# A mixture of experts behind two attentions: eight fixed tiles, seven looked up, and two tiles' weights loaded early

## The chip, the core and the metric

The kernel runs on one core of a Trainium2 chip. The metric is the device time of one execution in microseconds (us), and less is better. The core has TensorE (PE, matmuls and transposes), VectorE (DVE), ScalarE (ACT), GpSimd (POOL), and SyncE (SP), which issues nearly all transfers here. Each runs its own instruction list in order and meets the others at semaphores. All transfers share 16 DMA engines.

## The reference, cut to what matters

Four batches of 128 tokens with 512 features go through three stages, each added to its input: cross-attention over 2048 context rows per batch, self-attention over the 128 tokens, and a mixture of eight experts, of which each token takes two.

```python
x = x + xattn(layernorm(x), ctx_1024, ...)     # 16 heads, 2048 keys per batch
x = x + attn(layernorm(x), ...)                # 16 heads, rotary, 128 keys
x = x + ffn(layernorm(x), ...)

# ffn, xf = its input as 512 rows of 512
rn = (xf - mu) * rsqrt(var + EPS) * ln_gamma + ln_beta
probs = softmax(rn @ gate_w.T)
rw, sel = top_k(probs, 2)
comb = sum(one_hot(sel, 8) * rw[..., None], axis=1)
h = gelu(einsum('nc,efc->enf', xf, w1))        # w1: 8 x 1024 x 512
y = einsum('enf,ecf->enc', h, w2)              # w2: 8 x 512 x 1024
out = einsum('enc,ne->nc', y, comb)
```

## The kernel before

**Three stages.** `cross_attention` runs batch by batch; every engine has a loop (`Fori(0, NB - 1)`) over three batches, with semaphore counts and addresses computed in registers, and the fourth batch written out behind it. `self_attention` is written out and pipelined over the four batches. `mixture` follows it behind a block boundary.

**Tiles of the mixture.** The 1024 (token, expert) pairs are sorted by expert into slots of DRAM, `slots_in`, in tiles of 128 rows. Each expert begins a tile of its own, so 15 tiles always suffice (`TILES`). The router on VectorE works out each pair's slot (`rows`, semaphore `rowed`) and each tile's expert (`of_tile`, semaphore `tabled`). GpSimd scatters the normalised tokens with eight indirect transfers (`sent`). SyncE reads the 15 expert numbers into registers behind `tabled`, and addresses the weights with them.

**One tile k.** Its weights are 2 MB of w1 and 2 MB of w2 in float32. ScalarE makes the float16 high part (`w1_high`, `w2_high`, two instructions each) and VectorE the low part (`w1_low`, `w2_low`, two each). TensorE transposes the tile's 128 rows (`rows_transposed`, called the transposes below), and multiplies by w1 in 96 matmuls (the up part) and by w2 in 24 (the down part, `down_tile`). ScalarE applies the gelu to the up part's result, `y_evict` copies the down part's, and `y_store` sends it to `slots_out`. At the end GpSimd gathers both rows of each token, VectorE adds them, and the result is stored.

**Buffers and orders.** Raw weights, high and low parts, `rows_in`, `xT`, `h` and `y` are each double: tile k uses buffer k % 2. The order on TensorE, which the change leaves alone, is up(k), transposes(k + 1), down(k - 1). ScalarE in iteration k: w1_high(k + 1), y_evict(k - 2), gelu and high part of h for the two halves, x_high(k + 1), w2_high(k). VectorE follows it: w1_low(k + 1), the low parts of h, x_low(k + 1), w2_low(k). SyncE in iteration k, one queue:

```python
w1_load(k + 2)   # waits for w1_low(k)
rows_load(k + 2) # waits for the transposes of tile k
y_store(k - 2)   # waits for y_evict(k - 2)
w2_load(k + 2)   # waits for w2_low(k)
```

`w2_high(k)` waits for down(k - 2), which is the last reader of its buffer (`act.wait_ge(down, k - 1)`), and `y_evict(k)` for down(k). w1 and w2 of tile 0 are loaded during self-attention, and w1 of tile 0 is split there (in eight parts). w2 of tile 0 is split in the mixture.

**Lines.** SyncE: w1_load L1456, w2_load L1462, rows_load L1468, y_store L1472, output L1491. ScalarE: w1_high L1653 (the profile writes `w_hi<-w_raw`), w2_high L1661 (`cT_hi<-w_raw`: the high part of w2 lies in the old context buffer), x_high L1666, y_evict L1673, gelu L1686, high part of h L1690. VectorE: w1_low L1599, w2_low L1606 (`cT_lo<-w_raw`), x_low L1612, low part of h L1622. TensorE: transposes L1703, up L1751 to L1753, down L1734 to L1736. GpSimd: scatter L1509, gather L1517. L748 are the transposes at the start of a batch of cross-attention.

Of the kernel before, what the change touches and what calls it, by code (L numbers as in the profile page):

```python
# [16 lines left out]
P = 128  # L17
NB = 4
# [151 lines left out]
def cross_attention(nc, io, t, s):  # L170
# [19 lines left out]
    with ExitStack() as ctx:  # L190
# [103 lines left out]
        def _(sp):  # L294
# [75 lines left out]
            with sp.Fori(0, NB - 1) as b:  # L370
                one_batch(b, in_loop)
# [6 lines left out]
        def _(pool):  # L378
# [55 lines left out]
            with pool.Fori(0, NB - 1) as b:  # L434
                one_batch(b, in_loop)
# [3 lines left out]
        def _(v):  # L439
# [182 lines left out]
            with v.Fori(0, NB - 1) as b:  # L622
                one_batch(b, in_loop)
# [3 lines left out]
        def _(act):  # L627
# [109 lines left out]
            with act.Fori(0, NB - 1) as b:  # L737
                one_batch(b, in_loop)
# [3 lines left out]
        def _(pe):  # L742
# [177 lines left out]
            with pe.Fori(0, NB - 1) as b:  # L920
                one_batch(b, in_loop)
# [8 lines left out]
def self_attention(nc, io, t, s):  # L930
# [7 lines left out]
    with ExitStack() as ctx:  # L938
# [139 lines left out]
        def _(v):  # L1078
# [47 lines left out]
            def split_w1(n):  # L1126
# [3 lines left out]
                                               in0=t.w1_raw[:, c, half].rearrange("p c n -> p (c n)"), scalar=W_SCALE,  # L1130
# [83 lines left out]
        def _(act):  # L1214
# [8 lines left out]
            for step in STEPS:  # L1223
# [39 lines left out]
                if step == NB - 1:  # L1263

                    act.wait_ge(s.w1_in, 16)
                    for n in range(NF):
                        c_, half = w1_part(n)
                        nc.scalar.activation(t.w1_hi[:, c_, half], t.w1_raw[:, c_, half], ACT.Copy,
# [96 lines left out]
TILES = 2 * TOK // P + EXPERTS - 1  # L1365
# [3 lines left out]
def mixture(nc, io, t, s):  # L1369
# [3 lines left out]
    with ExitStack() as ctx:  # L1373
# [7 lines left out]
        w1_raw, w2_raw = [t.w1_raw, sb("w1_raw1", [P, NC, FF])], [t.w2_raw, sb("w2_raw1", [P, NF, D])]  # L1381
# [13 lines left out]
        counting = sb("m_counting", [P, TILES + NB * EXPERTS])  # L1395
# [4 lines left out]
        n_tiles, ends, starts = sb("m_n_tiles", [P, EXPERTS]), sb("m_ends", [P, EXPERTS]), sb("m_starts", [P, EXPERTS])  # L1400
        ones, over = sb("m_ones", [P, EXPERTS]), sb("m_over", [P, TILES, EXPERTS - 1])
        place, placed = sb("m_place", [P, NB, EXPERTS]), sb("m_placed", [P, 2, NB, EXPERTS])
        rows_f, of_tile_f = sb("m_rows_f", [P, 2, NB]), sb("m_of_tile_f", [P, TILES])
        rows = sb("m_rows", [P, 2, NB], mybir.dt.uint32)
        of_tile = sb("m_of_tile", [P, TILES], mybir.dt.int32)
        tile_no, rank = counting[:, 0:TILES], counting[:, TILES:].rearrange("p (b e) -> p b e", e=EXPERTS)

# [10 lines left out]
        w1_in, w2_in = [s.w1_in, sem("m_w1_in1")], [s.w2_in, sem("m_w2_in1")]  # L1418
# [27 lines left out]
        def _(sp):  # L1446
# [3 lines left out]
            sp.wait_ge(tabled, 1)  # L1450
            expert = [0] + [sp.value_load(of_tile[0:1, k:k + 1], min_val=0, max_val=EXPERTS - 1) for k in range(1, TILES)]

            def w1_load(k):
                if k >= 2:
                    sp.wait_ge(w1_lo_s, w1_parts(k - 2))
                sp.dma_start(w1_raw[k % 2][:, :, :], io.w1[bass.ds(expert[k], 1), :, :, :].rearrange("e p c n -> (e p) c n")  # L1456
                             ).then_inc(w1_in[k % 2], 16)

            def w2_load(k):
                if k >= 2:  # L1460
                    sp.wait_ge(w2_lo_s, PARTS * (k - 1))
                sp.dma_start(w2_raw[k % 2][:, :, :], io.w2[bass.ds(expert[k], 1), :, :, :].rearrange("e p c n -> (e p) c n")  # L1462
                             ).then_inc(w2_in[k % 2], 16)
# [405 lines left out]
```

## Time and profile before

| | us |
|---|---|
| median of 3 runs | 1163.97 |
| lowest, highest | 1159.47, 1173.82 |
| the profiled execution's own time | 1163.01 |
| its span, first to last instruction | 1161.1 |

| engine | busy us | share of the span |
|---|---|---|
| TensorE matmul | 950.7 | 82% |
| VectorE | 727.9 | 63% |
| ScalarE | 527.1 | 45% |
| GpSimd | 281.6 | 24% |
| DMA engines, mean (q1, which SyncE feeds) | | 33.9% |

Shares are averages over three stages: cross-attention takes the first 780 us, self-attention goes to 890, and the mixture takes the last 271 us. Times within the span are counted from its start, and what lies outside it is 1163.01 - 1161.1 = 1.9 us. The granted clock of TensorE averages 0.919 over the span.

### The profile page before, as it was taken

How to read it: one execution, taken by the hardware profiler on the slowest of the kernel's cores; microseconds unless marked ns; L12 is line 12 of the kernel's file. 1: busy time of each engine (PE TensorE's matmuls, PEld its weight loads, DVE VectorE, ACT ScalarE, POOL GpSimd, SP SyncE). 2: the span in 40 equal slices, each digit the busy share in tenths (PEclk: the TensorE clock that was granted, in tenths of full speed). 3: DMA queues.
4: the chain of work that ended last, by engine and by line, in shares of the span. 5: the costliest groups of instructions: out<-in, count | busy, mean ns of one | idle time of the engine just before them, and what ended most of it. 6: DMA issues, size and time to landing. Idle time of an engine off the chain costs nothing. (4 is left out here: it accounts for less than half of the span.)

```text
span 1161.1 us, 21099 instructions
## 1 busy us (share of the span) xinstructions
PE 950.7 (82%) x8057; PEld 529.9 (46%) x8057; DVE 727.9 (63%) x1066; ACT 527.1 (45%) x790; POOL 281.6 (24%) x244
## 2 busy tenths in 40 slices
PE   5899988889998889999889998757865078888871
PEld 4554444544443544444444444333443066555550
DVE  7965466683655673656683456775764277778772
ACT  4343444434344433344543344433453167778770
POOL 2610444320333410034530033442311200000002
PEclk9899998899999689999999999679977579999996
DMA  6333222032322013412123312218000558899844
GB/s 244 96 91 80 69 56 56 2 105 62 91 56 54 3 58 89 106 30 51 37 66 114 77 31 52 67 47 307 1 1 4 205 225 349 345 352 353 345 184 126
DMA packets 48531, 136.10 MB, mean 117 GB/s; under 512 B 9708, under 2 KB 11500, under 8 KB 44600
## 3 DMA queue, kind: packets, MB, share of 16 engines
q1 hardware_dynamic: 47160, 130.58, 33.9%
q0 software_dynamic: 1280, 4.20, 1.2%
q8 instruction: 71, 1.16, 0.4%
q14 instruction: 20, 0.16, 0.0%
HBM read 96.96 MB, written 11.04 MB: 93 GB/s over the span
## 5 line engine op out<-in xcount | busy, mean ns | idle before, releaser
L561 DVE TENSOR_REDUCE mpart<-ps_r 128x1 f32<-128x512 f32 x192 | 127.0, 687 | 96.1 <-PE ps_r L858 95.8
L693 ACT ACTIVATE pT<-ps_s 128x1024 f32<-128x1024 f32 x128 | 128.3, 1020 | 95.0 <-PE ps_s L880 91.3
L429 POOL TENSOR_TENSOR acc_pool<-acc_pool,pT 128x1024 f32<-128x1024 f32 x60 | 143.3, 2388 | 9.7 <-POOL acc_pool L429 5.5
L895 PE MATMUL ps_o<-pT,vals 128*32 128x128 f32 x2048 | 108.5, 305 | 24.3 <-ACT pT L693 24.0
L429 POOL TENSOR_TENSOR acc_pool<-pT 128x1024 f32<-128x1024 f32 x16 | 38.2, 2390 | 293.2 <-ACT pT L693 278.8
L554 DVE TENSOR_TENSOR k_lo<-k_f,k_hi 128x512 f16<-128x512 f32 x64 | 43.9, 688 | 103.8 <-ACT k_hi L715 103.8
L1751 PE MATMUL ps_h<-m_xT_hi,w_hi 128*128 128x128 f16 x480 | 84.9, 224 | 24.2 <-DVE m_xT_lo L1612 24.2
L769 PE MATMUL ps_r<-wv_hi,cT_hi 128*128 128x512 f16 x256 | 99.6, 389 | 6.0 <-DVE cT_lo L469 5.7
L839 PE MATMUL ps_r<-cT_hi,wk_hi 128*128 128x512 f16 x256 | 97.3, 380 | 5.1 <-DVE mpart L561 4.7
L710 ACT ACTIVATE k_f<-ps_r,kbias 128x512 f32<-128x512 f32 x64 | 43.9, 686 | 123.2 <-PE ps_r L841 120.7
L770 PE MATMUL ps_r<-wv_lo,cT_hi 128*128 128x512 f16 x256 | 99.2, 388 | 0.0
L771 PE MATMUL ps_r<-wv_hi,cT_lo 128*128 128x512 f16 x256 | 98.9, 386 | 0.0
L858 PE MATMUL ps_r<-k_stack,q_stack 98*128 98x512 f16 x192 | 84.1, 438 | 16.9 <-DVE mpart L561 12.7
L841 PE MATMUL ps_r<-cT_hi,wk_lo 128*128 128x512 f16 x256 | 97.0, 379 | 0.0
L840 PE MATMUL ps_r<-cT_lo,wk_hi 128*128 128x512 f16 x256 | 97.0, 379 | 0.0
L636 ACT ACTIVATE vals<-ps_r 128x512 f32<-128x512 f32 x64 | 38.2, 597 | 121.5 <-PE ps_r L771 121.5
L880 PE MATMUL ps_s<-q_stack,k_stack 98*128 (+1 forms) x1024 | 89.8, 233 | 2.2 <-ACT q_stack L720 2.2
L1752 PE MATMUL ps_h<-m_xT_lo,w_hi 128*128 128x128 f16 x480 | 84.7, 224 | 0.0
L1753 PE MATMUL ps_h<-m_xT_hi,w_lo 128*128 128x128 f16 x480 | 84.7, 224 | 0.0
L880 PEld LDWEIGHTS ps_s<-q_stack,k_stack 98*128 98x128 f16 x1024 | 70.8, 104 | 30.2 <-issue 21.3
L1599 DVE SCALAR_TENSOR_TENSOR w_lo<-w_raw,w_hi 128x2048 f16<-128x2048 f32 x28 | 62.9, 2288 | 31.0 <-ACT w_hi L1653 31.0
L895 PEld LDWEIGHTS ps_o<-pT,vals 128*32 128x32 f32 x2048 | 49.5, 116 | 69.6 <-issue 34.4
(233 smaller groups left out, 1849.3 us busy)
## 6 DMA issues: line engine op xcount, KB each, us to landing
w_raw<-in_w SPq DMA_DIRECT2D x30, 2048.0 KB, 10.1
raw<-in_context SPq DMA_DIRECT2D x64, 256.0 KB, 2.8
k_stack<-k_hi SPq DMA_DIRECT2D x256, 64.0 KB, 2.0
k_stack<-k_lo SPq DMA_DIRECT2D x128, 64.0 KB, 2.0
slots_in<-a_zeros SPq DMA_DIRECT2D x1, 3840.0 KB, 24.6
rows_in<-slots_in SPq DMA_DIRECT2D x15, 256.0 KB, 12.9
slots_out<-m_y SPq DMA_DIRECT2D x15, 256.0 KB, 10.5
q_stack<-k_stack SPq DMA_DIRECT2D x12, 128.0 KB, 2.3
```

Source lines behind the costliest of these rows:

```text
L429: nc.gpsimd.tensor_tensor(acc_pool[:, :], pT[:, 0, :] if p == 1 else acc_pool[:, :], pT[:, p % PT, :], ALU.add).then_inc(pool_add, 1)
L561: nc.vector.tensor_reduce(mpart[:, j, kb:kb + 1], p1_bank(step, n - 1), AX.X, ALU.max).then_inc(p1_max, 1)
L693: nc.scalar.activation(pT[:, p % PT, :], ps_s[p % 2][:, :], ACT.Exp, scale=SM_SCALE).then_inc(exp_done, 1)
L769: nc.tensor.matmul(bank[:, :], cT_hi[:, c, keys], t.wv_hi[:, c, :], start=(c == 0), stop=False)
L770: nc.tensor.matmul(bank[:, :], cT_hi[:, c, keys], t.wv_lo[:, c, :], start=False, stop=False)
L771: last = nc.tensor.matmul(bank[:, :], cT_lo[:, c, keys], t.wv_hi[:, c, :], start=False, stop=(c == NC - 1))
L839: nc.tensor.matmul(bank[:, :], t.wk_hi[:, c, col], cT_hi[:, c, keys], start=(c == 0), stop=False)
L840: nc.tensor.matmul(bank[:, :], t.wk_hi[:, c, col], cT_lo[:, c, keys], start=False, stop=False)
L841: last = nc.tensor.matmul(bank[:, :], t.wk_lo[:, c, col], cT_hi[:, c, keys], start=False, stop=(c == NC - 1))
L880: last = nc.tensor.matmul(ps_s[p % 2][:, at:at + P], t.k_stack[g % 2][0:ROWS, j, P * kt:P * (kt + 1)], t.q_stack[0:ROWS, HPG * g + j, bass ...
L895: last = nc.tensor.matmul(ps_o[g % 2][HD * j:HD * (j + 1), 0:P], vals[:, 2 * p + i, head:head + HD], pT[:, p % PT, at:at + P], start=(p == ...
L1751: nc.tensor.matmul(to, w1_hi[u][:, c, col], xT_hi[u][:, c, :], start=(c == 0), stop=False)
```

## The change

There are still 15 tiles. Tiles 0 to 7 now belong to experts 0 to 7, fixed when the kernel is built, and only tiles 8 to 14 (`MORE` = 7) are looked up: an expert with over 128 pairs has its further tiles there. The router's arithmetic for a pair's slot gets four more small instructions (one on 8 values, three on 32), and its table of experts 7 entries instead of 15.

The weights of tiles 0 and 1 are loaded during self-attention, behind the zeroing of `slots_in` (before: those of tile 0, ahead of it). In the mixture ScalarE splits w2(0), w1(1) and w2(1) early, in between the router's steps. ScalarE's order in iteration k is now y_evict(k - 2), w2_high(k), gelu, x_high(k + 1), w1_high(k + 2); VectorE's is w2_low(k), low parts of h, x_low(k + 1), w1_low(k + 2). SyncE issues w1(2) and w2(2) before the rows, w1(3) and w2(3) behind rows 0 and 1, then reads the seven expert numbers, and in iteration k loads rows of tile k + 2, w1 of tile k + 4, stores y of tile k - 2, and loads w2 of tile k + 4. The order on TensorE is as it was.

The loop over three batches of cross-attention is written out on all five engines. The diff, cut:

```diff
...
-            with pe.Fori(0, NB - 1) as b:
+            for b in range(NB - 1):
                 one_batch(b, in_loop)
...
             sp.dma_start(t.gate[:, :, :], io.gate).then_inc(s.gate_in, 16)
-            sp.dma_start(t.w1_raw[:, :, :], io.w1[0:1, :, :, :].rearrange("e p c n -> (e p) c n")).then_inc(s.w1_in, 16)
-            sp.dma_start(t.w2_raw[:, :, :], io.w2[0:1, :, :, :].rearrange("e p c n -> (e p) c n")).then_inc(s.w2_in, 16)
             sp.wait_ge(zeroed, 1)
             sp.dma_start(io.slots_in.rearrange("(n p) d -> p n d", p=P),
                          zeros[:, :].unsqueeze(1).broadcast_to([P, TILES, D])).then_inc(s.slots_zeroed, 16)
+            for e in range(2):
+                sp.dma_start(t.w1_raw[e][:, :, :], io.w1[e:e + 1, :, :, :].rearrange("e p c n -> (e p) c n")
+                             ).then_inc(s.w1_in[e], 16)
+                sp.dma_start(t.w2_raw[e][:, :, :], io.w2[e:e + 1, :, :, :].rearrange("e p c n -> (e p) c n")
+                             ).then_inc(s.w2_in[e], 16)
...
-TILES = 2 * TOK // P + EXPERTS - 1
+MORE = 2 * TOK // P - 1
+TILES = EXPERTS + MORE
...
-            sp.wait_ge(tabled, 1)
-            expert = [0] + [sp.value_load(of_tile[0:1, k:k + 1], min_val=0, max_val=EXPERTS - 1) for k in range(1, TILES)]
+            expert = list(range(EXPERTS))
+
+            def experts_of_further_tiles():
+                sp.wait_ge(tabled, 1)
+                expert.extend(sp.value_load(of_tile[0:1, k:k + 1], min_val=0, max_val=EXPERTS - 1) for k in range(MORE))
+
+            def weights_of(w, k):
+                e = expert[k]
+                return (w[e:e + 1, :, :, :] if k < EXPERTS else w[bass.ds(e, 1), :, :, :]).rearrange("e p c n -> (e p) c n")
 
             def w1_load(k):
-                if k >= 2:
-                    sp.wait_ge(w1_lo_s, w1_parts(k - 2))
-                sp.dma_start(w1_raw[k % 2][:, :, :], io.w1[bass.ds(expert[k], 1), :, :, :].rearrange("e p c n -> (e p) c n")
-                             ).then_inc(w1_in[k % 2], 16)
+                sp.wait_ge(w1_lo_s, w1_parts(k - 2))
+                sp.dma_start(w1_raw[k % 2][:, :, :], weights_of(io.w1, k)).then_inc(w1_in[k % 2], 16)
 
             def w2_load(k):
-                if k >= 2:
-                    sp.wait_ge(w2_lo_s, PARTS * (k - 1))
-                sp.dma_start(w2_raw[k % 2][:, :, :], io.w2[bass.ds(expert[k], 1), :, :, :].rearrange("e p c n -> (e p) c n")
-                             ).then_inc(w2_in[k % 2], 16)
+                sp.wait_ge(w2_lo_s, PARTS * (k - 1))
+                sp.dma_start(w2_raw[k % 2][:, :, :], weights_of(io.w2, k)).then_inc(w2_in[k % 2], 16)
 
             def rows_load(k):
                 if k >= 2:
@@ -1471,19 +1480,23 @@
                 sp.wait_ge(y_out, k + 1)
                 sp.dma_start(io.slots_out[P * k:P * (k + 1), :], y[k % 2][:, :]).then_inc(y_sent[k % 2], 16)
 
-            w1_load(1)
-            w2_load(1)
+            w1_load(2)
+            w2_load(2)
             sp.wait_ge(sent, 16 * 2 * NB)
             rows_load(0)
             rows_load(1)
+            w1_load(3)
+            w2_load(3)
+            experts_of_further_tiles()
             for k in range(TILES):
                 if k + 2 < TILES:
-                    w1_load(k + 2)
                     rows_load(k + 2)
+                if k + 4 < TILES:
+                    w1_load(k + 4)
                 if k >= 2:
                     y_store(k - 2)
-                if k + 2 < TILES:
-                    w2_load(k + 2)
+                if k + 4 < TILES:
+                    w2_load(k + 4)
...
-            then_wait(nc.vector.tensor_scalar(n_tiles[:, :], total, float(P), 1.0, ALU.is_gt, ALU.add))
+            then_wait(nc.vector.tensor_scalar(n_more[:, :], total, float(P), None, ALU.is_gt))
             for k in (2, 3):
-                then_wait(nc.vector.scalar_tensor_tensor(out=n_tiles[:, :], in0=total, scalar=float(P * k),
-                                                         in1=n_tiles[:, :], op0=ALU.is_gt, op1=ALU.add))
-            then_wait(nc.vector.tensor_tensor_scan(ends[:, :], ones[:, :], n_tiles[:, :], 0.0, ALU.mult, ALU.add))
-            then_wait(nc.vector.tensor_tensor(starts[:, :], ends[:, :], n_tiles[:, :], ALU.subtract))
-            then_wait(nc.vector.tensor_scalar(starts[:, :], starts[:, :], float(P), None, ALU.mult))
+                then_wait(nc.vector.scalar_tensor_tensor(out=n_more[:, :], in0=total, scalar=float(P * k),
+                                                         in1=n_more[:, :], op0=ALU.is_gt, op1=ALU.add))
+            then_wait(nc.vector.tensor_tensor_scan(ends[:, :], ones[:, :], n_more[:, :], 0.0, ALU.mult, ALU.add))
+            then_wait(nc.vector.tensor_tensor(shift[:, :], ends[:, :], n_more[:, :], ALU.subtract))
+            then_wait(nc.vector.tensor_scalar(shift[:, :], shift[:, :], EXPERTS - 1.0, float(P), ALU.add, ALU.mult))
+            then_wait(nc.vector.tensor_tensor(shift[:, :], shift[:, :], first_slot, ALU.subtract))
+            then_wait(nc.vector.tensor_scalar(behind[:, :, :], ps_c[:, 0:NB, :], float(P), None, ALU.is_ge))
+            then_wait(nc.vector.tensor_tensor(behind[:, :, :], behind[:, :, :],
+                                              shift[:, :].unsqueeze(1).broadcast_to(wide), ALU.mult))
             then_wait(nc.vector.tensor_tensor(place[:, :, :], ps_c[:, 0:NB, :],
-                                              starts[:, :].unsqueeze(1).broadcast_to(wide), ALU.add))
+                                              first_slot.unsqueeze(1).broadcast_to(wide), ALU.add))
+            then_wait(nc.vector.tensor_tensor(place[:, :, :], place[:, :, :], behind[:, :, :], ALU.add))
...
+            w2_low(0)
+            w1_low(1)
+            w2_low(1)
             x_low(0)
             for k in range(TILES):
-                if k + 1 < TILES:
-                    w1_low(k + 1)
+                if k >= 2:
+                    w2_low(k)
                 for i in range(2):
                     v.wait_ge(h_hi_s, 2 * k + i + 1)
                     nc.vector.scalar_tensor_tensor(out=h_lo[k % 2][:, NC * i:NC * (i + 1), :], in0=h_f[:, i, :, :],
@@ -1624,7 +1645,8 @@
                                                    op0=ALU.mult, op1=ALU.subtract).then_inc(h_lo_s, 1)
                 if k + 1 < TILES:
                     x_low(k + 1)
-                w2_low(k)
+                if k + 2 < TILES:
+                    w1_low(k + 2)
...
-            act.wait_ge(g_tr, NB)
-            for c in range(NC):
-                last = nc.scalar.activation(gT[:, c, :], ps_x[1][:, P * c:P * (c + 1)], ACT.Identity,
-                                            bias=affine[:, 1, c:c + 1], scale=affine[:, 0, c:c + 1])
-            last.then_inc(g_out, 1)
-            act.wait_ge(chain, 3)
-            nc.scalar.activation(prob[:, :, :], prob[:, :, :], ACT.Exp).then_inc(g_exp, 1)
-
-            def w1_high(k):
+            def w1_high(k, parts=range(PARTS)):
                 act.wait_ge(w1_in[k % 2], 16 * uses(k))
                 if k >= 2:
                     act.wait_ge(up, 2 * (k - 1))
-                for i in range(PARTS):
+                for i in parts:
                     nc.scalar.activation(w1_split(w1_hi[k % 2], i), w1_split(w1_raw[k % 2], i), ACT.Copy,
                                          scale=W_SCALE).then_inc(w1_hi_s, 1)
 
@@ -1673,12 +1687,21 @@
                 nc.scalar.activation(y[k % 2][:, :], ps_y[k % 2][:, :], ACT.Copy, scale=UNSCALE).then_inc(y_out, 1)
 
             w2_high(0)
+            w1_high(1, (0,))
+            act.wait_ge(g_tr, NB)
+            for c in range(NC):
+                last = nc.scalar.activation(gT[:, c, :], ps_x[1][:, P * c:P * (c + 1)], ACT.Identity,
+                                            bias=affine[:, 1, c:c + 1], scale=affine[:, 0, c:c + 1])
+            last.then_inc(g_out, 1)
+            w1_high(1, (1,))
+            act.wait_ge(chain, 3)
+            nc.scalar.activation(prob[:, :, :], prob[:, :, :], ACT.Exp).then_inc(g_exp, 1)
+            w2_high(1)
             x_high(0)
             for k in range(TILES):
-                if k + 1 < TILES:
-                    w1_high(k + 1)
                 if k >= 2:
                     y_evict(k - 2)
+                    w2_high(k)
                 for i in range(2):
                     act.wait_ge(up, 2 * k + i + 1)
                     if k:
@@ -1691,8 +1714,8 @@
                                          scale=A_SCALE).then_inc(h_hi_s, 1)
                 if k + 1 < TILES:
                     x_high(k + 1)
-                if k:
-                    w2_high(k)
+                if k + 2 < TILES:
+                    w1_high(k + 2)
...
-        t.w1_raw, t.w2_raw = sb("w1_raw", [P, NC, FF]), sb("w2_raw", [P, NF, D])
+        t.w1_raw, t.w2_raw = [sb(f"w1_raw{u}", [P, NC, FF]) for u in range(2)], [sb(f"w2_raw{u}", [P, NF, D]) for u in range(2)]
...
```

## Rows read from the trace of the kernel before

**Rows 1.** The page's slices: 40 of 29 us each, in tenths; DMA too.

```profile
PE   5899988889998889999889998757865078888871
DMA  6333222032322013412123312218000558899844
```

**Rows 2.** Windows: length, busy us (and count) of each engine, clock, DMA share, GB/s.

```profile
1028.00:1042.00 14.00, 12.22 (x145) 9.08 (x143) 11.46 (x8) 10.51 (x10) 0.00 (x0) 1.00 0.90 347
1044.00:1046.00 2.00, 2.00 (x11) 0.91 (x10) 1.74 (x1) 2.00 (x3) 0.00 (x0) 1.00 1.04 434
```

**Rows 3.** The chain that ended last, one turn of it: start, us, what.

```profile
1042.24 13.15 DMA w_raw<-in_w
...
1062.39 1.81 ACT cT_hi L1661
1064.22 4.51 DVE cT_lo L1606 x2
1068.75 0.34 SPq L1462
```

**Rows 4.** Timeline of SyncE's queue: start, us, engine, line.

```profile
1041.72 0.34 SPq L1462 DMA_DIRECT2D w_raw<-in_w  x1
1042.24 0.87 SPq L1456 DMA_DIRECT2D w_raw<-in_w  x1
1055.64 0.34 SPq L1462 DMA_DIRECT2D w_raw<-in_w  x1
```

**Rows 5.** The waits of SyncE's queue from 900 us: total, times, longest.

```profile
SPq L1462 <- DVE cT_lo L1606: 119.0, 13, 15.7
```

**Rows 6.** Timeline of all engines, one tile.

```profile
1030.14 0.72 SPq L1468 DMA_DIRECT2D rows_in<-slots_in  x1
1042.31 3.71 ACT L1653 ACTIVATE w_hi<-w_raw 128x2048 f16<-128x2048 f32 x2 [3.35 <-DMA w_raw<-in_w]
1043.00 0.66 PE L1703 MATMUL ps_x<-ident_sb,rows_in 128*128 128x128 f32 x4 [0.78 <-DMA rows_in<-slots_in]
1043.49 0.38 PE L1734 MATMUL ps_y<-cT_hi,h_hi 128*128 128x512 f16 x1
1048.46 0.38 PE L1736 MATMUL ps_y<-cT_hi,h_lo 128*128 128x512 f16 x1
1050.61 0.23 PE L1751 MATMUL ps_h<-m_xT_hi,w_hi 128*128 128x128 f16 x1 [1.78 <-DVE m_xT_lo L1612]
1055.93 0.22 PE L1753 MATMUL ps_h<-m_xT_hi,w_lo 128*128 128x128 f16 x1
```

**Rows 7.** The view of L1462's instructions, the loads of w2: issue to landing, us.

```profile
DMA to landing us min/median/max: 7.8/8.5/12.6
```

**Rows 8.** DMA issues by line: KB each, median us to landing.

```profile
raw<-in_context SPq DMA_DIRECT2D x64, 256.0 KB, 2.8
```

**Rows 9.** The waits of TensorE up to 780 us: total, times, longest.

```profile
PE ps_s L748 <- issue: 6.2, 2, 3.3
```

**Rows 10.** Timeline of all engines, the start of the mixture.

```profile
907.69 0.17 DVE L1594 CAST m_of_tile<-m_of_tile_f 128x15 int32<-128x15 f32 x1
917.56 0.35 SPq L1456 DMA_DIRECT2D w_raw<-in_w  x1
925.99 0.81 SPq L1468 DMA_DIRECT2D rows_in<-slots_in  x2
931.40 1.11 PE L1703 MATMUL ps_x<-ident_sb,rows_in 128*128 128x128 f32 x4 [26.57 <-DMA rows_in<-slots_in]
933.93 0.29 PE L1751 MATMUL ps_h<-m_xT_hi,w_hi 128*128 128x128 f16 x1 [1.42 <-DVE m_xT_lo L1612]
```

**Rows 11.** Windows of the start, as rows 2.

```profile
930.00:935.00 5.00, 2.18 (x15) 1.79 (x16) 0.71 (x2) 2.45 (x3) 0.00 (x0) 0.50 1.06 443
935.00:940.00 5.00, 5.00 (x63) 5.00 (x62) 4.47 (x2) 4.08 (x4) 0.00 (x0) 0.66 0.33 131
```

**Rows 12.** Timeline of all engines, the end of the mixture.

```profile
1139.33 0.60 ACT L1673 ACTIVATE m_y<-ps_y 128x512 f32<-128x512 f32 x1 [7.29 <-PE ps_y L1736]
```

More of the change, by code:

```diff
@@ L432, in one_batch @@
                             pool.wait_ge(pool_add, b * sum(POOL_ADDS) + n_add)
-            with pool.Fori(0, NB - 1) as b:
+            for b in range(NB - 1):
                 one_batch(b, in_loop)
@@ L620, in one_batch @@
                                                        op1=ALU.subtract).then_inc(s.self_lo, 1)
-            with v.Fori(0, NB - 1) as b:
+            for b in range(NB - 1):
                 one_batch(b, in_loop)
@@ L735, in one_batch @@
                                              scale=W_SCALE).then_inc(s.self_hi, 1)
-            with act.Fori(0, NB - 1) as b:
+            for b in range(NB - 1):
                 one_batch(b, in_loop)
@@ L918, in one_batch @@
                         last.then_inc(op_mm, 1)
-            with pe.Fori(0, NB - 1) as b:
+            for b in range(NB - 1):
                 one_batch(b, in_loop)
@@ L1263, in _ @@
                 if step == NB - 1:
[L1265 removed]
+                    act.wait_ge(s.w1_in[0], 16)
                     for n in range(NF):
                         c_, half = w1_part(n)
[L1268 removed]
+                        nc.scalar.activation(t.w1_hi[:, c_, half], t.w1_raw[0][:, c_, half], ACT.Copy,
                                              scale=W_SCALE).then_inc(s.w1_hi, 1)
@@ L1399, in mixture @@
         chosen = sb("m_chosen", [P, NB + 1, EXPERTS], F16)
-        n_tiles, ends, starts = sb("m_n_tiles", [P, EXPERTS]), sb("m_ends", [P, EXPERTS]), sb("m_starts", [P, EXPERTS])
-        ones, over = sb("m_ones", [P, EXPERTS]), sb("m_over", [P, TILES, EXPERTS - 1])
+        n_more, ends, shift = sb("m_n_more", [P, EXPERTS]), sb("m_ends", [P, EXPERTS]), sb("m_shift", [P, EXPERTS])
+        ones, over = sb("m_ones", [P, EXPERTS]), sb("m_over", [P, MORE, EXPERTS - 1])
+        behind = sb("m_behind", [P, NB, EXPERTS])
         place, placed = sb("m_place", [P, NB, EXPERTS]), sb("m_placed", [P, 2, NB, EXPERTS])
-        rows_f, of_tile_f = sb("m_rows_f", [P, 2, NB]), sb("m_of_tile_f", [P, TILES])
+        rows_f, of_tile_f = sb("m_rows_f", [P, 2, NB]), sb("m_of_tile_f", [P, MORE])
         rows = sb("m_rows", [P, 2, NB], mybir.dt.uint32)
-        of_tile = sb("m_of_tile", [P, TILES], mybir.dt.int32)
-        tile_no, rank = counting[:, 0:TILES], counting[:, TILES:].rearrange("p (b e) -> p b e", e=EXPERTS)
+        of_tile = sb("m_of_tile", [P, MORE], mybir.dt.int32)
+        tile_no, first_slot = counting[:, 0:MORE], counting[:, MORE:MORE + EXPERTS]
+        rank = counting[:, MORE + EXPERTS:].rearrange("p (b e) -> p b e", e=EXPERTS)
         ps_h = [ctx.enter_context(nc.psum_tensor(f"ps_h{i}", [P, NC, P], F32)) for i in range(2)]
@@ L1590, in _ @@
             then_wait(nc.vector.tensor_tensor(
-                over[:, :, :], ends[:, 0:EXPERTS - 1].unsqueeze(1).broadcast_to([P, TILES, EXPERTS - 1]),
-                tile_no.unsqueeze(2).broadcast_to([P, TILES, EXPERTS - 1]), ALU.is_le))
+                over[:, :, :], ends[:, 0:EXPERTS - 1].unsqueeze(1).broadcast_to([P, MORE, EXPERTS - 1]),
+                tile_no.unsqueeze(2).broadcast_to([P, MORE, EXPERTS - 1]), ALU.is_le))
             then_wait(nc.vector.tensor_reduce(of_tile_f[:, :], over[:, :, :], AX.X, ALU.add))
@@ L1796, in program @@
         t.logits = sb("logits", [P, NB, EXPERTS])
-        s.gate_in, s.w1_in, s.w2_in, s.w1_hi, s.w1_lo = [
-            ctx.enter_context(nc.semaphore(name))
-            for name in ("m_gate_in", "m_w1_in", "m_w2_in", "m_w1_hi", "m_w1_lo")]
+        s.gate_in, s.w1_hi, s.w1_lo = [ctx.enter_context(nc.semaphore(name)) for name in ("m_gate_in", "m_w1_hi", "m_w1_lo")]
+        s.w1_in, s.w2_in = [[ctx.enter_context(nc.semaphore(f"m_{w}_in{u}")) for u in range(2)] for w in ("w1", "w2")]
         s.m_st, s.m_var, s.m_powed, s.m_normed, s.g_tr, s.g_out, s.g_mm = [
@@ L1856 @@
         "before": np.ascontiguousarray(np.stack([np.triu(np.ones((P, P)), 1), np.ones((P, P))], axis=1).astype(np.float16)),
-        "counting": np.tile(np.concatenate([np.arange(TILES), np.tile(EXPERTS - np.arange(EXPERTS), NB)]),
-                            (P, 1)).astype(np.float32),
+        "counting": np.tile(np.concatenate([np.arange(MORE), P * np.arange(EXPERTS),
+                                            np.tile(EXPERTS - np.arange(EXPERTS), NB)]), (P, 1)).astype(np.float32),
     }
```

9 lines of the change are left out of this document (4 added, 5 removed).

## The prediction, made before the change was run

> **What bounds the kernel now.** I read the page's slices first: until 780 us TensorE is busy and the DMA engines are at 1 to 4 tenths; from slice 33 on (958 us) the DMA engines are at 8 and 9 tenths and TensorE at 8 [rows 1]. The change is nearly all in this last part, so the windows of a tile come next. One tile took 13.5 us (13.9 from one issue of w2 to the next, 13.1 to the one after, 1068.75 [rows 3, 4]). In a stretch of 14 us ScalarE was busy 10.5, VectorE 11.5, TensorE 12.2 and the DMA engines 0.90 of the time at 347 GB/s, while they reach 434 GB/s once they have enough queued [rows 2]. So none of the four is full: 4.72 MB for a tile (4.19 of weights, 0.26 of rows, 0.26 of y) would take 10.9 us at 434 GB/s. What closes the turn is a ring, which the chain shows: the transfer of w2 and w1 (13.15 us), then work on the tile up to `w2_high` and `w2_low`, and with its end the next issue of w2 [rows 3]. The timeline of SyncE says the same: w1 and then the rows go out right behind w2, since one queue issues them in order [rows 4], and that queue waits 119.0 us in 13 waits for `w2_low` [rows 5]. The place to look for trouble in the new order is thus SyncE's wait for `w2_low`, and what is queued behind it.
>
> **Cross-attention written out.** What is seen of the loop on TensorE are two idle times without a releaser ahead of L748, 6.2 us together, at the two backward branches [rows 9]. TensorE is the busy engine there, so they are worth their length: -6.2 us. If a straight list has fetches of its own at these places, it is 0; the register arithmetic that goes as well lies beside matmuls, and I count nothing for it.
>
> **Self-attention.** 4 MB more are loaded, and all 8 MB behind the zeroing. There is plenty of slack: the DMA engines rest for three slices in the middle of self-attention [rows 1]. Cost 0; were w1(0) late for its split, it would be some us. In the mixture's start ScalarE now does w2(0) and a half of w1(1), three instructions of 1.9 us (3.71 for two) [rows 6], before it waits for the router's transposes, for which it idled before. Cost 0.
>
> **Start of the mixture.** Four more router instructions cost 0.85 us: the last table stood at 907.9, and now at 908.7. Before, SyncE issued weights at 917.6 behind 14 register loads, 9.7 us, and those weights held up the scatter until 926.0, when rows 0 and 1 went out; TensorE began at 931.4 [rows 10]. Now w1(2) goes out at once, and w2(2) behind `w2_low(0)`: 908.7 + 4.5 = 913.2. It lands 7.8 us later or more [rows 7], at 921.1, which also bounds what the scatter shares with it. Rows 0 then land at about 923.5. Transposes, x_high and x_low (1.1 + 0.6 + 0.7, with gaps) start up(0) at 926.0; it runs at a low clock at first, as before, and takes 7.7, until 933.7. Gelu, high part, x_high and x_low (2.7) start up(1) at 936.4; up takes 5.3 (1050.61 to 1055.93), transposes 0.7 and down 5.2 [rows 6]. So down(0) ends at 936.4 + 5.3 + 0.7 + 5.2 = 947.6, say 948, give or take 4. So far the change gains about 7 us.
>
> **The new turn.** Here I find a wait that the new order makes. In SyncE's queue rows(k + 3), in iteration k + 1, stand behind w2(k + 4), in iteration k. That one waits for `w2_low(k + 2)`, which follows `w2_high(k + 2)`, which ScalarE does only after y_evict(k), which waits for down(k). TensorE needs rows(k + 3) for its transposes between up(k + 2) and down(k + 1). So each down part waits for rows that are issued only after the down part before it. Before, rows(k + 2) stood behind w2(k + 1), which waited for `w2_low(k - 1)`, two tiles earlier. The weights got four tiles of lookahead, and the rows kept two but stand in the same queue.
>
> The turn, from the end of one down part to the next:
> - y_evict 0.1 + 0.6 [rows 12], the first half of `w2_high` 1.9 with its start, `w2_low` 4.5, SyncE's step 0.05 [rows 3]: 7.15 us to the issue of w2.
> - rows behind w2 in the same queue. In rows 6 the rows of a tile were usable 0.7 us after w1 that was issued ahead of them (1042.31 and 1043.00), so they come in order behind the weights. w2 takes 7.8 to 8.5 from issue to landing [rows 7], partly behind what was left of the batch before; rows of 0.25 MB add 0.6 at 434 GB/s. Now the queue is empty when w2 is issued, so from below: 2.8 us for 0.25 MB alone [rows 8] and 4.8 for 2 MB less the 0.6 that one contains twice, some 6.8. I take 8.0, between 6.8 and 9.1.
> - transposes 0.7 and down 5.2 at the full clock, 0.05 to start: 5.95. `w1_high(k + 2)` and `w1_low(k + 2)` lie beside that down part and end about with it, so they add nothing.
>
> That is 21.1 us. up(k + 2), 5.3 us, runs inside the wait, and TensorE then idles about 10 us in each turn. For that the clock pays: after 26.6 us of rest before the first transposes the clock stood at 0.50 until some point between 935 and 940, about 4.5 to 5 us after steady work began at 933.93 [rows 10, 11]. Work at half the clock for 4.8 us costs 2.4. Bounds: 0, if 10 us of rest don't lower it, and 5.9, if the 5.9 us run wholly at 1.2 instead of 2.4 GHz. I take 2.4, since the rest is long against the gap of 1.78 us after which rows 6 still show full speed (L1753, 0.22). So p = 21.1 + 2.4 = 23.5, between 19.9 and 28.1.
>
> The page "TensorE: Matmul & The Clock Gate" of the Trainium skill, section "HAM oscillation", describes a kernel whose matmuls wait for a transfer in each round and restart at the low clock in every one. By that rule the cost recurs in each turn, as assumed; no stretch of this trace repeats a rest of 10 us, so the trace neither confirms it nor speaks against it.
>
> **How often.** w2(k + 4) exists up to k = 10. The gated rows are those of tiles 3 to 13, eleven turns, from the end of down(0) to the end of down(11). Then up(13), transposes, down(12), up(14), down(13), down(14): 5.4 + 0.7 + 5.2 + 5.4 + 5.2 + 5.2 = 27.1. From the end of down(14) at 1139.3 to the end of the span there were 21.8 [rows 12], unchanged. Sum: 948 + 11 x 23.5 + 27.1 + 21.8 - 6.2 = 1249.2 of span; outside the span lie 1.9. This gives 1251 us against the profiled execution's 1163.01, which stands 1.0 under the median. In short the time is 992.6 + 11 p.
>
> **Rivals.**
> - The clock stays at half for the whole of each transposes-and-down stretch: p = 21.1 + 5.9 = 27.0, time 1289.6, slower still. For it: rest fills nearly half of each turn. Against: busy stretches of 5 us sufficed at the start. Chance 0.12.
> - Rows don't stand behind w2 in the DMA engines, and land 2.8 us after their issue at 7.15 + 0.5: p = 10.45 + 5.95 = 16.4, with 2.4 for the clock 18.8. Time 1173 to 1199. Against it is the 0.7 us between w1 and rows in rows 6 and a landing of rows with the weights in every tile. The Trainium skill, page "DMA: Bandwidth & Descriptors", section "Queues, rings and completion order", says that descriptors of one ring are taken in ring order but that completion is not strictly so; with it alone, the rows would still start behind w2. Chance 0.06, half of it within 2%.
> - The other side, faster: the wait never decides, since w2's early split frees its buffer in time (I have read an order wrongly, or rows are usable earlier), and the lookahead of four tiles lets each engine run on. Then TensorE decides, with 5.3 + 0.7 + 5.2 = 11.2 and small waits, say 11.8 a tile; ScalarE's 10.5 and 10.9 for the transfers lie under it. With 4 for the waits of the last tile, and 21.8 - 6.2 + 1.9 = 17.5 as above, the time would be 948 + 14 x 11.8 + 4 + 17.5 = 1135. It decides once w2 and rows are issued 8.0 - 5.3 = 2.7 us before down(k) ends, that is, not behind a wait for something that follows down(k). Against it is the queue's order. Chance 0.06.
> - The same, but the turn stays as it was, at 13.5: 948 + 14 x 13.5 + 4 + 17.5 = 1158, no difference. Chance 0.04.
>
> **The numbers.** The forecast has 0.72, and its own bounds for p give 1211 to 1302. A measurement of this kernel tells changes of about 2% (23 us) from none. Slower by over 2%: 0.72 + 0.12 + 0.03 = 0.87; within 2%: 0.03 + 0.04 = 0.07; faster: 0.06. The range 1205 to 1292 leaves out the faster and equal cases and most of the rows' rival, 0.15 in all, and the slowest end of the clock.
>
> **What would show it.** In the profile after: TensorE's wait for `rows_in` (L1703 before) at eleven places of about 10 us, 110 us in all, where it was 0.8 a tile; SyncE issues w2 and rows half a us apart, 7 us after each down part; the DMA engines at about half in the mixture's slices; the turn from down to down 23.5 us; matmuls of the down part at the slow pace at the start of each; first transposes of the mixture at about 917 to 918 (923.5 less 6.2); no idle time at the two batch boundaries. Wrong would be the prediction if the rows land before up(k + 2) ends, which a small wait for `rows_in` would show, or if p differs: each us of it is 11 us of the time.

## The result, and the profile after

The changed kernel takes 1254.63 us (median of 4 runs, 1253.92 to 1258.49), where the kernel before takes 1164.41: a ratio of 1.077 with a 95% interval of 1.070 to 1.084. The forecast was 1251. The profiled execution took 1254.57, its span is 1252.8.

The slices of the page of after, as rows 1, with the clock. In the mixture (slices 31 to 37 here, 34 to 38 before) TensorE is at 4 to 6 tenths where it was at 8, the DMA engines are at 3 to 6 where they were at 8 and 9, and the clock is at 6 to 8:

```profile
PE   5799988999988999989998867875166466456583
PEclk9799999999999999979999867997577678878887
DMA  6333121222221331202422225500463553564423
```

The waits of TensorE from 900 us (total, times, longest). Twelve waits for rows, the first of them at the start; the other eleven are 111 us. None is for weights:

```profile
PE ps_x L1726 <- DMA rows_in<-slots_in: 135.9, 12, 24.9
```

SyncE's queue in the timeline, two turns. L1472 is w2, L1477 rows, L1468 w1, L1481 y. In each turn the rows go out 0.4 us behind w2. Before, the same three went out together too [rows 4, 6], but at the release by `w2_low(k - 1)`:

```profile
1019.68 0.33 SPq L1472 DMA_DIRECT2D w_raw<-in_w  x1
1020.06 0.43 SPq L1477 DMA_DIRECT2D rows_in<-slots_in  x1
1020.70 0.35 SPq L1468 DMA_DIRECT2D w_raw<-in_w  x1
...
1043.58 0.34 SPq L1472 DMA_DIRECT2D w_raw<-in_w  x1
1043.97 0.43 SPq L1477 DMA_DIRECT2D rows_in<-slots_in  x1
```

The chain, one turn of the ring, answers to rows 3. `w2_high`, both halves of `w2_low`, the rows' transfer (8.01), transposes at the slow pace (1.11), and a down part that begins at 0.43 a matmul, twice the 0.22 of the full clock:

```profile
1037.12 1.91 ACT cT_hi L1675
1039.06 4.50 DVE cT_lo L1624 x2
1043.97 8.01 DMA rows_in<-slots_in
1052.02 1.11 PE ps_x L1726 x4
1053.13 0.43 PE ps_y L1757
```

From the last matmul of one down part to that of the next the starts are 24.3, 24.0, 24.0, 23.9, 24.0, 23.8, 23.9, 24.0, 24.0, 23.8 and 24.3 us apart, eleven turns, mean 24.0; then 11.0, 10.5 and 5.2. Before, the same count gives 11.5 once and then 13 to 15.

### The profile page after: what moved, and what is told of

Read it like the earlier page. It is cut to its first block and busy times, and to the rows that moved or that the text cites. A ratio compares the mean times of both kernels' runs of the same rounds, so it can differ in the third digit from the quotient of the medians.

```text
span 1252.8 us, 19687 instructions
## 1 busy us (share of the span) xinstructions
PE 964.9 (77%) x8057; PEld 533.1 (43%) x8057; DVE 725.4 (58%) x1070; ACT 530.6 (42%) x790; POOL 289.2 (23%) x244
## 5 line engine op out<-in xcount | busy, mean ns | idle before, releaser
L895 PE MATMUL ps_o<-pT,vals 128*32 128x128 f32 x2048 | 105.0, 298 | 25.6 <-ACT pT L693 25.5
L1726 PE MATMUL ps_x<-ident_sb,rows_in 128*128 128x128 f32 x60 | 15.2, 402 | 135.9 <-DMA rows_in<-slots_in 135.9
L858 PE MATMUL ps_r<-k_stack,q_stack 98*128 98x512 f16 x192 | 81.8, 426 | 16.0 <-DVE mpart L561 13.1
L1624 DVE SCALAR_TENSOR_TENSOR cT_lo<-w_raw,cT_hi 128x2048 f16<-128x2048 f32 x30 | 67.4, 2288 | 36.9 <-ACT cT_hi L1675 36.9
L880 PE MATMUL ps_s<-q_stack,k_stack 98*128 98x128 f16 x1024 | 86.3, 228 | 1.9 <-ACT q_stack L720 1.9
L1530 POOL DMA_INDIRECT m_back<-slots_out,m_rows x8 | 8.6, 1081 | 325.6 <-DMA slots_out<-m_y 323.5
## 6 DMA issues: line engine op xcount, KB each, us to landing
w_raw<-in_w SPq DMA_DIRECT2D x30, 2048.0 KB, 11.5
```

Source lines behind the costliest of these rows:

```text
L895: last = nc.tensor.matmul(ps_o[g % 2][HD * j:HD * (j + 1), 0:P], vals[:, 2 * p + i, head:head + HD], pT[:, p % PT, at:at + P], start=(p == ...
L1624: nc.vector.scalar_tensor_tensor(out=w2_split(w2_lo[k % 2], i), in0=w2_split(w2_raw[k % 2], i), scalar=W_SCALE, in1=w2_split(w2_hi[k % 2], ...
```

## The experiments

All are compared with the kernel before on the same chip. Kernels that were measured on different chips are set against each other by their ratios.

**e1: only the loops written out.** The edit, in each of the five engines, on the kernel before:

```diff
-            with pe.Fori(0, NB - 1) as b:
+            for b in range(NB - 1):
```

> The kernel before with only the five loops of cross-attention written out; the mixture is that of before. In the trace of after the mixture began 14 us earlier, where 6.2 had been forecast. Theory A: writing out is worth the two idle times at the branches and some register work, 6 to 8 us, and the rest of the 14 was the clock, which stood at 0.5 in two stretches of 17 us near the ends of two batches before (194 and 375 us) and in one after (535 us), by chance. Then the median falls by 6 to 8 us against before, 1157, with single runs scattered by some 8 us either way. Theory B: the loop itself brings the low clock on, and writing out takes it away in every run: 14 us, 1150. In both the turn of the mixture stays at 13.5 us.

Measured: 1156.17 us, ratio 0.991 (0.987 to 0.995), 12 runs from 1148.11 to 1165.7. The two waits at the branches [rows 9] are gone from TensorE's list of waits. The interval is 6 to 16 us and holds both numbers; what separates the theories is the clock. Windows at the end of the first two batches in the trace of e1 (its clock is the number after the five engines):

```profile
200.00:210.00 10.00, 9.60 (x75) 4.14 (x74) 7.55 (x12) 2.05 (x2) 0.18 (x1) 0.50 0.00 0
370.00:380.00 10.00, 8.24 (x57) 3.48 (x57) 7.83 (x11) 2.58 (x3) 7.98 (x4) 0.57 0.20 49
```

The same place of the first batch in after, and of the third:

```profile
200.00:210.00 10.00, 8.09 (x125) 4.79 (x124) 7.49 (x11) 4.53 (x6) 1.06 (x2) 1.00 0.00 0
540.00:550.00 10.00, 9.94 (x74) 3.89 (x73) 6.83 (x10) 2.05 (x2) 2.30 (x1) 0.50 0.01 2
```

75 and 74 matmuls in 10 us at the low clock (0.50, 1.2 GHz), 125 at the high one (2.4 GHz). The low stretch comes in some batches and not in others, with loops and without. So theory B falls: writing out doesn't take it away. The 14 us by which the mixture began earlier in after are the branches and a lucky draw of such stretches. The other traces tell how much is which. Twelve kernels here have the written-out loops, and in their traces the router's transposes start anywhere from 877.0 us (e2) to 890.2 (e5). In e4 and e7 the granted clock from 100 to 700 us is 0.95, as in before; there they start at 890.1 and 888.4, 5.4 and 7.1 us earlier than before's 895.5. In after that clock is 0.98, and they start at 881.2. So the branches are worth about the 6.2 of the forecast, and the other 8 of the 14 were luck of the clock.

**e2: rows ahead of w2.** On after, SyncE's order alone:

```diff
+            rows_load(2)
             for k in range(TILES):
-                if k + 2 < TILES:
-                    rows_load(k + 2)
                 if k + 4 < TILES:
                     w1_load(k + 4)
                 if k >= 2:
                     y_store(k - 2)
+                if k + 3 < TILES:
+                    rows_load(k + 3)
                 if k + 4 < TILES:
                     w2_load(k + 4)
```

> The kernel after, with one change of order on SyncE: rows(k+3) are issued ahead of w2(k+4), in iteration k, instead of behind it. Theory: the rows' wait is the gate of the turn, so TensorE's wait for rows_in goes. What is late next is the store of y: y(k-1) still stands behind w2(k+4) and w1(k+5), lands some 12.6 us after w2's issue, and y_evict(k+1) waits for it: a turn of 0.6 + 1.9 + 4.5 + 0.05 + 12.6 = 19.7 us instead of 24.05, so 1254.6 - 11 x 4.35 = 1207. Rival, that y's store has slack enough and the engines' own work decides at once: a turn of about 12, time 1135. Rival, that the rows weren't the gate but the weights' landing: no change, 1254.

Measured: 1203.64 us, ratio 1.031 (1.025 to 1.038). The steady turn is 20.5 (forecast 19.7). ScalarE's waits in its trace name the gate that took over, the copy of y, which waits for an earlier y to be stored; the chain that ended last runs through that store in every steady turn:

```profile
ACT m_y L1688 <- DMA slots_out<-m_y: 93.1, 10, 10.8
```

```profile
1052.87 1.91 ACT cT_hi L1676
1054.80 4.50 DVE cT_lo L1625 x2
...
1060.23 12.51 DMA slots_out<-m_y
```

So the rows were the gate of after, and a second one of nearly the same size lay right behind it, in the same queue. One thing that was expected did not come: TensorE still waited 62.9 us in ten waits for rows behind the first. They now leave behind w2(k + 3), w1(k + 4) and y, and land 12.6 us after their issue (median), but beside the wait for y, which closes the turn.

**e3: rows and y ahead of w2.** As e2, with `rows_load(k + 3)` and `y_store(k - 1)` both between w1(k + 4) and w2(k + 4).

> The kernel after, with rows(k+3) and y(k-1) both issued ahead of w2(k+4). Theory: nothing that TensorE or ScalarE needs soon stands behind SyncE's wait for w2_low any more, the lookahead of four tiles works, and TensorE's own work with small waits decides, a turn of 11.8 to 12.3: down(0) ended at 940.4 in the trace of after, + 14 x 11.8 to 12.3 + 4 + 23.7 around the end gives 1133 to 1140. Rival, that the turn of 13.5 before came from the transfers' rate itself: 1157, as before less the start's gain. Rival, that a further order decides: between 1157 and 1254.

Measured: 1152.12 us, ratio 0.986 (0.979 to 0.993): faster than the kernel before by 1.4%, less than the 2% that the prediction took as the least that can be told, and 12 us and more short of the theory. Turns alternate, 11.0 and 16.6 to 19.0. TensorE's waits, and the queue:

```profile
PE ps_x L1726 <- DMA rows_in<-slots_in: 49.4, 7, 25.0
```

```profile
1005.94 0.35 SPq L1472 DMA_DIRECT2D w_raw<-in_w  x1
1006.48 0.34 SPq L1468 DMA_DIRECT2D w_raw<-in_w  x1
1006.87 0.43 SPq L1477 DMA_DIRECT2D rows_in<-slots_in  x1
```

The rows now leave at w2's release with w1 ahead of them too: 4 MB instead of 2, 13.1 us from issue to landing (median). They are still late in every second tile. I had put them ahead of w2(k + 4), and overlooked that w1(k + 4), issued ahead of them, itself stood behind w2(k + 3).

**e5: rows and y first of all.** The order in iteration k is rows(k + 3), y(k - 1), w1(k + 4), w2(k + 4).

> The kernel after, with SyncE's order in iteration k: rows(k+3), y(k-1), w1(k+4), w2(k+4). In e3 rows stood behind w1 and so behind 4 MB, and TensorE waited for them some 5 us in every second tile, a mean turn of 12.8 and of 14.6 in the middle. Theory: here they stand behind 2 MB only, land 8.6 us after w2's issue, in time for any turn over 10.5; next comes w1, which lands 13.2 after w2's issue and is wanted at 2 turns less 11.8: a turn of 12.5 or under. With the end of down(0) at 940.4 + 14 x 12.3 + 4 + 23.7 that is 1140, 12 us under e3 and 2.5% under the kernel before. Rival, that the transfers' rate decides the turn in e3 (332 GB/s in its slices, as before): no change against e3, 1152.

Measured: 1134.5 us, ratio 0.974 (0.968 to 0.979). Twelve turns are 12.6 on average. So the rate of the transfers wasn't what held e3. What ScalarE waits for next is w1:

```profile
ACT w_hi L1666 <- DMA w_raw<-in_w: 23.8, 10, 4.0
```

**e8: rows and y from GpSimd's queue.** On after, `rows_load` and `y_store` move to GpSimd between scatter and gather; SyncE issues only weights.

```diff
-            sp.dma_start(rows_in[k % 2][:, :], io.slots_in[P * k:P * (k + 1), :]) ...
+            nc.gpsimd.dma_start(rows_in[k % 2][:, :], io.slots_in[P * k:P * (k + 1), :]) ...
```

> The kernel after, with all loads of rows and stores of y issued by GpSimd, which has nothing else to do between scatter and gather; SyncE's queue holds weights only. Nothing waits in program order behind w2_low's wait but weights. Theory: the gate is a matter of one queue's order, so it goes without any reordering, and rows and y share the DMA engines with the weights instead of standing behind them: the turn of e5 or less, 12.1 to 12.5, time 1135 to 1142, if GpSimd's issue of a transfer costs it about 1 us as its scatters do. Rival, that transfers issued there land late when the engines are full of weights, as the last scatter before, which took 7.5 us: still about 12.5, since they are issued early. Rival, that it is slower than e3 (1152): its queue is taken up by waits for y while rows could go.

Measured: 1140.9 us, ratio 0.980 (0.974 to 0.985). Another queue does what the reordering did, to about half a per cent: the place in the queue made the gate. An issue there took 0.55 us, not 1. Twelve turns are 12.3 on average, even shorter than e5's. What e8 loses lies at the start: its first transposes come 43.2 us behind the router's, where it is 34.3 in after. SyncE, which no longer waits for the scatter, issues w1(3) and w2(3) beside it (907.4 and 911.8). Rows 0 and 1 leave only at 925.6, 10.4 us behind the last issue of the scatter (1.8 in after).

**e7: the gate put into the old order.** On e1, with two tiles of lookahead:

```diff
                 if k + 2 < TILES:
                     w1_load(k + 2)
-                    rows_load(k + 2)
                 if k >= 2:
                     y_store(k - 2)
                 if k + 2 < TILES:
                     w2_load(k + 2)
+                    rows_load(k + 2)
```

> e1 (the kernel before with the loops written out, 1156 us) with one change: rows(k+2) are issued behind w2(k+2), which waits for w2_low(k), instead of ahead of it. Everything else is of before, with its two tiles of lookahead. Theory: rows behind the wait for w2_low are enough to make a gate in any order. Its ring here: rows(k+2) 8.6 us behind w2's issue, transposes 0.7, x_high and w2_high's first half 2.7, w2_low 4.5, 0.1: 16.6 instead of 13.5, 13 times, so 1156 + 40 = 1196. Rival, that rows behind weights matter only with the lookahead of four tiles: 1156.

Measured: 1197.84 us, ratio 1.026 (1.018 to 1.033), so 3.5% over e1, 41 us. The mean of twelve turns is 16.7, forecast 16.6. TensorE waits 79.1 us in 14 waits for rows, where it waited 34.8 in e1. The gate doesn't need the lookahead of four tiles.

**e4 and e6: is the low clock a term of the turn?** On after, constants are multiplied in each gated wait (they add nothing to the result), 80 matmuls in e4 and 92 in e6:

```diff
             def rows_transposed(k):
+                for n in range(80 if 3 <= k <= TILES - 2 else 0):
+                    nc.tensor.matmul(ps_g[:, 0:2 * P], before[:, 1, :], before[:, :, :]..., start=True, stop=True)
```

> The kernel after, with 80 matmuls of constants (N = 256, into a bank nobody reads) on TensorE ahead of each of the eleven gated transposes: 80 x 0.107 = 8.6 us of work inside a wait of 10 us. Nothing else is changed. Theory: the wait's second price is the clock; with TensorE kept busy it stays at 1.00, transposes take 0.66 instead of 1.12, down 5.2 instead of about 7.6, and the turn falls from 24.05 to 21.1 to 21.4: 1254.6 - 11 x 2.8 = 1224. Rival, that the turn is set by rows alone and the clock is no term of it: no change, or slower if the matmuls run late into the transposes.

Measured: 1253.59 us, ratio 1.072 (1.066 to 1.078): no change. The trace shows why it was no test: 1.9 to 3.4 us of rest remained in each turn, and the clock was still low for 3.4 us or more in nine of the eleven stretches of transposes and down part. The mean turn was 23.7.

> As e4, with 92 instead of 80 matmuls in each gated wait. e4 showed no gain: its trace has 2.0 us of rest left in each turn and the clock still at 0.50 for 3.4 us of the down part, so that it ended only about 1 us sooner, and the rows landed 8.7 instead of 8.0 us after their issue. With 92 the rest is 0.5 us or less. Theory A: the clock then stays at 1.00, transposes and down take 5.9 instead of 8.6 (7.5 in e4), and the turn falls from 24.05 to 21.4 to 22: 1254 - 11 x 2.4 = 1228. Theory B: something else holds the turn near 23.7 (rows land later by what the down part gains): 1250 to 1254 again.

Measured: 1242.61 us, ratio 1.066 (1.058 to 1.074), between the theories. Windows of 40 us of after:

```profile
1040.00:1080.00 40.00, 20.14 (x171) 12.97 (x169) 17.06 (x13) 17.06 (x18) 0.00 (x0) 0.76 0.58 231
```

and of e6, where the clock stays at 1.00 through all eleven filled turns:

```profile
1040.00:1080.00 40.00, 36.74 (x341) 28.54 (x339) 17.21 (x13) 15.53 (x15) 0.00 (x0) 1.00 0.62 237
```

Transposes and down part take 5.8 us (1050.39 to 1056.23) where after takes 8.5, which would give 2.7 us a turn. The turn fell from 24.0 to 22.7. Half of the gain came back as other waits: rows landed 8.8 us after their issue instead of 7.9 (medians), and y's store, e2's gate, showed itself in ScalarE's waits:

```profile
ACT m_y L1687 <- DMA slots_out<-m_y: 14.9, 9, 1.8
```

Why the rows land 0.9 later when TensorE is kept busy isn't explained. It is not their place in the queue: w2 ahead of them lands later too, 8.5 us after its issue instead of 7.7 (medians), and e4's rows are as late as e6's (8.8). So the clock is a term of after's turn, worth 2.7 us alone and 1.3 as things stood.

**e9 and e10: why the mixture's start gained so little.** In after GpSimd's issues of the scatter (start, us):

```profile
894.82 2.90 POOL L1522 DMA_INDIRECT slots_in<-m_normed_x,m_rows  x1 [14.08 <-DVE m_rows L1606]
898.02 1.61 POOL L1522 DMA_INDIRECT slots_in<-m_normed_x,m_rows  x1 [0.31 <-issue]
899.94 1.89 POOL L1522 DMA_INDIRECT slots_in<-m_normed_x,m_rows  x1 [0.30 <-issue]
...
908.74 0.98 POOL L1522 DMA_INDIRECT slots_in<-m_normed_x,m_rows  x1 [0.30 <-issue]
```

VectorE's early splits, six instructions of 2.25 us, run from 894.3 to 907.6, and the issues come one in 2.2 us until just then. e10 is after with one line more, e9 is e5 with the splits moved:

```diff
# e10
+            v.wait_ge(sent, 16 * 2 * NB)
             w2_low(0)
             w1_low(1)
             w2_low(1)
             x_low(0)
# e9
+            w2_low(0)
             v.wait_ge(g_mm, NB)
...
-            w2_low(0)
+            v.wait_ge(sent, 16 * 2 * NB)
             w1_low(1)
-            w2_low(1)
             x_low(0)
+            w2_low(1)
```

> The kernel after with one line more: VectorE waits for the scatter's end before w2_low(0). This is for its trace, not its time: w2(2) is issued only 4.5 us behind the scatter. If VectorE slows the scatter, all eight issues take 0.97 to 1.3 us as before; if the weights' transfers do, they would be short here too, so that e9, in which w2(2) lands before or during the scatter, is to be read beside it. The start of up(0) moves from 918.1 to about 919.5, the turn of 24 stays: 1254 to 1260.

> e5 (1134.5 us) with VectorE's early splits moved: w2_low(0) into its 4.7 us of rest before the router's logits, w1_low(1) behind a wait for the whole scatter, then x_low(0), then w2_low(1). In every kernel that splits beside the scatter, GpSimd takes 1.6 to 2.9 us for an indirect issue while VectorE works on 128x2048 values, and 0.97 while it rests; the scatter's issues there take 16.2 us instead of 10.2, and TensorE's first transposes come 34.3 us after those of the router, where 28 had been forecast. Theory A: the splits slow the scatter; without them the first transposes come some 7 us earlier (27 to 28 us behind the router's) and the time falls by about 7, to 1127.5, less what w1_low(1) and w2_low(1) now cost behind the scatter (w1_low(1) ends with the first transposes, nothing). Theory B: the weights of tile 2 in the DMA engines slow the scatter, not VectorE: issues still take 1.9 us, and no gain.

Measured: e10 took 1263.37 us in one run, over the 1254 to 1260 expected. All of its issues take 0.98 to 1.27 us. But w2(2) waits for `w2_low(0)`, which now follows the scatter, and rows 0 and 1 stand behind that load in the queue: the first transposes come 38.7 us behind the router's, 4.4 later than in after. e9 took 1130.44, ratio 0.967 (0.961 to 0.973) against e5's 0.974. Its first two issues:

```profile
892.61 1.27 POOL L1521 DMA_INDIRECT slots_in<-m_normed_x,m_rows  x1 [14.01 <-DVE m_rows L1613]
894.19 0.98 POOL L1521 DMA_INDIRECT slots_in<-m_normed_x,m_rows  x1 [0.31 <-issue]
```

That leaves theory B, the weights: w2(2) was issued 9.0 us before the scatter in e9 (883.61) and after it in e10 (916.57), so both move the weights away together with the splits. The trace of after parts the two. Its first issue of the scatter, the longest with 2.90 us, starts at 894.82, and w2(2) is issued only at 898.80; the last two, 0.98 and 0.97, run behind the splits with the DMA engines still at work. Windows of after (the fifth engine is GpSimd, the last two numbers are the share and GB/s of the DMA engines):

```profile
895.00:897.00 2.00, 0.00 (x0) 0.00 (x0) 2.00 (x2) 0.00 (x0) 2.00 (x1) 0.50 0.00 0
908.70:911.00 2.30, 0.00 (x0) 0.00 (x0) 0.00 (x0) 0.00 (x0) 1.95 (x2) 0.50 0.62 239
```

So it is VectorE that slows them. In e9 the first transposes come 28.3 us behind the router's, instead of 34.3 in after. The ratios of e9 and e5 differ by 0.7%, 8 us, but their intervals overlap, so the time alone would not show it. The Trainium skill, page "SBUF — State Buffer", section "SBUF: two separate sides", says that VectorE with two SBUF inputs and GpSimd reading SBUF take a shared port pair for a whole instruction each and block the other; one issue for each 2.25 us split is what that rule gives here. That the port is the cause rests on this fit; no run separates it from another way in which VectorE could hold up an issue.

**e11: w1 one tile earlier.** On e9, the order is rows(k + 3), y(k - 1), w1(k + 5), w2(k + 4):

```diff
             rows_load(2)
+            w1_load(4)
...
-                if k + 4 < TILES:
-                    w1_load(k + 4)
+                if k + 5 < TILES:
+                    w1_load(k + 5)
+                if k + 4 < TILES:
                     w2_load(k + 4)
```

> e9 with w1 issued one tile earlier on SyncE: in iteration k rows(k+3), y(k-1), w1(k+5), w2(k+4), so that w1 no longer stands behind w2's wait. In e5 ScalarE waited 23.8 us in ten waits for w1. Theory: the turn is 11.7 in e5 and TensorE's own work 11.2, so at most 0.5 x 14 = 7 us can come back, and the DMA engines need 10.9: 3 to 6 us under e9. Rival, that those waits lie beside TensorE's work and cost nothing: as e9. Rival, that w1 now goes ahead of the rows in the queue and they come late again: slower than e9.

Measured: 1121.4 us (6 runs, 1111.05 to 1127.07), ratio 0.959 (0.953 to 0.964), 0.8% under e9 and the fastest. The twelve turns from the first down part on are 11.8 on average, where they were 12.8 in e9; I had taken 11.7 for e5's turn from a rougher count, so more came back than the 3 to 6 expected. ScalarE no longer waits for w1. Windows of 40 us:

```profile
1000.00:1040.00 40.00, 38.10 (x405) 27.05 (x403) 36.68 (x27) 36.42 (x36) 0.00 (x0) 1.00 1.01 406
```

TensorE, VectorE, ScalarE and the DMA engines are all at 0.9 and over.

## Why the prediction was right, step by step

- **The gate.** Rows(k + 3) behind w2(k + 4), behind `w2_low(k + 2)`, behind down(k): shown. It occurs eleven times as counted; e2, e5 and e8 take it away by nothing but order or queue, and e7 makes the same kind of gate in the kernel of before.
- **The turn**, forecast 23.5, measured 24.0. From the end of the down part, 1036.6, to the issue of w2, 1043.6, are 7.0 (forecast 7.15). Rows landed 8.4 after w2's issue (8.0; the lower bound of 6.8 was a slip, its own terms 2.8 + 4.8 - 0.6 give 7.0). Transposes and down, 1052.0 to 1060.5, took 8.5 (5.95 + 2.4 = 8.35). The clock term rested on one stretch of rows 10 and 11; it held. The trace of after has a low stretch at each of the eleven down parts, and e6 has none. That agrees with the Trainium skill, page "TensorE: Matmul & The Clock Gate", section "HAM oscillation", where such a wait brings the low clock back in every round.
- **Cross-attention written out**, forecast 6.2. In this pair of traces the mixture starts 14.2 us earlier (the router's transposes at 881.24 instead of 895.47). e1 puts the edit at 6 to 16, and shows the clock's low stretches as a source of scatter of the same size. Against the traces of e4 and e7, at the same clock as before, it is 5 to 7. Mechanism and size were right; the other 8 us of this pair were luck.
- **The mixture's start**, forecast to bring the first transposes 7.9 us nearer to the router's (28.0 behind them instead of 35.9). They came 34.3 behind, a gain of 1.6. This step failed: the splits that I had costed as work beside the router made six of GpSimd's eight issues 1.6 to 2.9 us long instead of 0.97. I had counted the queue of each moved step, and put what it does to the engine beside it at nothing. e9 gives 28.3.
- **The sum.** Down(0) ended at 940.4 (941.8 forecast), eleven turns took 263.9 (258.5), the last tiles 26.7 (27.1), the end 21.8 (21.8). So the good agreement at down(0) is luck, two errors of opposite sign: 8 us gained in cross-attention by the clock and 6.3 lost in the start. Without the luck of the clock the total would have been 12 us off instead of 4.
- **The rivals.** The clock stayed low for a part of each transposes-and-down stretch, not for all of it. Rows did stand behind w2. The faster case, that four tiles of lookahead let the engines run on, was forecast at 1135 with 11.8 a tile; it needed rows and y out of the way, and e5 gives 1134.5 with 12.6 a tile, e11 the 11.8.

## What to carry to other kernels

When loads are issued further ahead, look at what stands behind them in the queue: a small transfer needed soon must not follow a wait for a buffer that only later work frees. Mending one gate uncovers the next in the same queue (rows, then y, then w1 here, 24.0, 20.5, 14 to 15, 12.6, 11.8 us a tile), so write the order by when each transfer's wait ends and when it is wanted. With an order that fits (e11) the kernel is 4% faster than the one before; about 1% of that is the loops of cross-attention (e1), and a part the moved splits (e9).

## What the runs showed of the hardware that wasn't expected

- An indirect transfer's issue on GpSimd takes 0.97 us (the first one 1.27) while VectorE rests and 1.6 to 2.9 beside instructions of VectorE with two float inputs of 128x2048 (e10, e9 against after and e5).
- In cross-attention the clock falls to 0.50 for some 14 to 24 us near the end of some batches and for 3.4 us or not at all near the end of others, in the same code; the matmuls there come at 0.6 of the rate (75 in 10 us instead of 125). Runs of one kernel spread by up to 20 us, those of after by 5.
- A rest of 1.9 to 3.4 us in each turn (e4) came with the low clock in nine of eleven down parts; rests of 0.5 to 2.8 us in e6, and of up to 2.1 before (from 950 us on), did not bring it. The two ranges overlap, so the length of the rest alone doesn't tell which.
